# Output projection applied per head, with rows added into x + bo in DRAM by accumulating scatters

## The reference, cut to what matters

```
q, k, v = x @ Wq + bq, x @ Wk + bk, x @ Wv + bv           # 16 heads of 16
scores  = q @ k.T * 0.25                                  # 4096 x 4096 for each head
top     = top_k(scores.max(-1) - scores.mean(-1), 307)
sel     = softmax(q[top] @ k.T * 0.25) @ v                # 307 x 16 for each head
a       = zeros; a[top] = sel
x1      = layernorm(x + (a @ Wo + bo))
xr, xk  = mu_r*x1 + (1-mu_r)*prev(x1), mu_k*x1 + (1-mu_k)*prev(x1)
out     = layernorm(x1 + sigmoid(xr @ W_r.T) * (relu(xk @ W_k.T)**2 @ W_v.T))
```

## Time and profile before

| | us |
|---|---|
| median of 3 runs | 3275.21 |
| lowest and highest run | 3268.93, 3281.18 |
| span of the profiled execution | 3267.6 |
| busy in it: TensorE, VectorE, ScalarE, GpSimd | 2972.6, 2890.4, 2836.5, 1580.4 |

### The profile page before, as it was taken

The page is one execution under the profiler, slowest core; times in us unless marked ns, Lnnn a source line. Parts: engine busy times, 40 slices in busy tenths (PEclk is TensorE's granted clock), DMA queues, the critical chain, the costliest instruction groups (busy, mean ns, idle before and its releaser), DMA issues. The chain is left out here.

```text
span 3267.6 us, 57726 instructions
## 1 busy us (share of the span) xinstructions
PE 2972.6 (91%) x15364; PEld 1367.2 (42%) x15364; DVE 2890.4 (88%) x5704; ACT 2836.5 (87%) x6246; POOL 1580.4 (48%) x2787
## 2 busy tenths in 40 slices
PE   6999899998989999998999999899999899997688
PEld 3333333333433443443334444444444343444477
DVE  4999999999989998998999999899999898997567
ACT  5999889997988999899899888799988699895566
POOL 4223122224644553654355564766565663557754
PEclk8999999999999999999999999999999999998889
DMA  6334223342151131223121233122151023202022
GB/s 182 90 86 121 76 71 81 90 34 40 34 38 31 35 41 17 32 40 35 24 41 30 60 52 40 36 39 41 37 48 41 24 39 32 41 15 16 16 83 73
DMA packets 263603, 163.56 MB, mean 50 GB/s; under 512 B 168876, under 2 KB 242796, under 8 KB 259180
## 3 DMA queue, kind: packets, MB, share of 16 engines
q1 hardware_dynamic: 255180, 156.41, 25.8%
q0 software_dynamic: 6144, 1.37, 0.5%
q10 hardware_dynamic: 1952, 2.10, 0.2%
HBM read 111.86 MB, written 47.86 MB: 49 GB/s over the span
## 5 line engine op out<-in xcount | busy, mean ns | idle before, releaser
L1189 DVE CUSTOM_DVE_ANT_0 JK<-DP,AB 128x1024 bf16<-128x1024 f32 x2048 | 2463.1, 1222 | 239.8 <-DVE SPr L1189 91.5
L1033 ACT ACTIVATE AB<-CP 128x512 f32<-128x512 f32 x4096 | 2291.3, 622 | 201.0 <-PE CP L749 147.0
L768 PE MATMUL DP<-KS,QS 128*128 128x512 f16 x4096 | 1230.2, 382 | 61.5 <-DVE SPr L1189 53.9
L1641 POOL TENSOR_TENSOR SCR<-E 128x307 f16<-128x307 f32 x957 | 666.1, 709 | 516.3 <-ACT E L1068 509.2
L749 PE MATMUL CP<-KS,QS 128*128 128x512 f16 x2048 | 789.7, 386 | 57.4 <-ACT AB L1033 34.6
L758 PE MATMUL CP<-KS,QS 128*128 128x512 f16 x2048 | 790.4, 386 | 34.8
L768 PEld LDWEIGHTS DP<-KS,QS 128*128 128x128 f16 x4096 | 357.0, 99 | 357.9 <-DVE SPr L1189 171.5
L1068 ACT ACTIVATE E<-BP 128x307 f32<-128x307 f32 x904 | 430.5, 476 | 34.5 <-PE BP L860 31.3
L749 PEld LDWEIGHTS CP<-KS,QS 128*128 128x128 f16 x2048 | 197.5, 96 | 525.3 <-ACT AB L1033 460.3
L758 PEld LDWEIGHTS CP<-KS,QS 128*128 128x128 f16 x2048 | 196.8, 96 | 411.5 <-ACT AB L1033 376.2
L860 PE MATMUL BP<-QT,KA 128*128 128x307 f16 x904 | 267.2, 296 | 22.6 <-ACT QT L1060 19.0
(11 more groups left out here) (414 smaller groups left out, 3087.2 us busy)
## 6 DMA issues: line engine op xcount, KB each, us to landing
KS<-KTC SPq DMA_DIRECT2D x256, 128.0 KB, 4.6
QS<-QSC SPq DMA_DIRECT2D x512, 64.0 KB, 2.2
KA<-KTC SPq DMA_DIRECT2D x128, 128.0 KB, 4.0
QN<-SCR SPq DMA_DIRECT2D x16, 544.0 KB, 3.4
SCR<-in_L_attn_x SPq DMA_DIRECT2D x16, 512.0 KB, 5.0
AO<-E SPq DMA_DIRECT2D x16, 512.0 KB, 6.9
VF<-in_L_attn_x SPq DMA_DIRECT2D x64, 128.0 KB, 2.2
VF<-AO SPq DMA_DIRECT2D x64, 128.0 KB, 2.2
```

The source lines that it names most:

```text
L768: r = pe.matmul(o[:, 512 * j:512 * j + 512], qs, ks[j][:, 0, :], start=True, stop=True)
L1033: act.activation(AB[p % 3][:, 512 * j:512 * j + 512], BANK["C%d" % j], ACT.Abs).then_inc(ab_full, 1)
L1189: dve.tensor_tensor_reduce(out=JK[p % 2][:], in0=BANK["D%d" % u], in1=AB[p % 3][:], scale=1.0, scalar=0.0, op0=ALU.add, op1=ALU.max, accum ...
L1641: pool.tensor_tensor(EL[a % NE], E[a % NE][:], EH[a % NE], ALU.subtract).then_inc(el_g, 1)
```

## The change

- `Wo` is applied head by head. The two copies of 16 rows of `Wo` that a head needs (for the high and the low half of the value sums) are loaded to `WB` by the sync engine. `otr` becomes two steps `wo`. Part 0 brings the softmax sums into columns (three products with one column of the identity) and multiplies the last 51 rows with `WB`; VectorE takes the reciprocal and scales. Part 1 multiplies the first 256 rows, and ScalarE scales them.
- `put` adds rows of 256 numbers to `Y` in DRAM by three accumulating indirect DMAs. `Y` holds x + bo: copied from x by sixteen DMAs of 512 KB (`ycopy`, in the steps of the values of sequence 0) and added to by sixteen accumulating DMAs from GpSimd (`ybias`, in the sixteen steps that transpose sequence 1). No zeros are written.
- The value bias is added in the value products, by one more product with a matrix of ones.
- `feed` has no Wo: it reads `Y`, and an iteration has seven steps. The first norm uses the same statistics as the second (`BN_STATS`).
- The mixing is written as `prev + mu*(cur - prev)`, with one subtraction, from one ring `x1R` instead of three tiles. In the second `feed` both scalings of the norms move from VectorE to ScalarE, and the addition before the second norm moves from VectorE to GpSimd.

```diff
-                yield [("otr", g, j // NT, bank()), ("put", g, j // NT)]
+                yield [("wo", g, j // NT, 0, bank())]
+                yield [("wo", g, j // NT, 1, bank()), ("put", g, j // NT)]
...
-            products = [("f7", 7, (("f3", 4), ("f2m", 3)), ()), ("f6", 6, (("f2s", 3),), (("f8", 8),)),
-                        ("f6k", 6, (("f2r", 3),), (("f9", 9),)),
-                        None, ("f2", 2, (), (("f0", 0),))]
...
+            products = [("f7", 7, (("f3", 4),), ()), ("f6", 6, (("f8", 8),), ()), ("f6k", 6, (("f2r", 3),), (("f9", 9),))]
...
+                    pe.wait_ge(bv_pool, 1)
+                    pe.matmul(o[:, 0:D], onesh[:], bvr[:], start=True, stop=False)
+                r = products(o[:, 0:D], "v", t, slice(0, D), False, part, False)
...
-            def otr(g, hl, bank):
+            def wo(g, hl, part, bank):
                 hx = HEAD0[g] + hl
-                o = claim(bank)
-                pe.wait_ge(ot_act, hx + 1)
-                for c in range(3):
-                    r = pe.transpose(o[:, 64 * c:64 * c + 2 * DH + 1], OT[hx % 2][:, 128 * c:128 * c + 128],
-                                     ident[0:2 * DH + 1, 0:2 * DH + 1])
-                r.then_inc(ot_pe, 1)
-                owed[bank] = ((og_dve, hx + 1),)
-
-            def f1(b, t, bank, late):
-                k = NT * b + t
-                o = claim(bank)
-                pe.wait_ge(l_f[k % 3], 32 * (k // 3 + 1))
-                transposes(o, 2, lambda q: fao[k % 3][:, 128 * q:128 * q + 128], ident[:]).then_inc(f_t0, 1)
-                owed[bank] = ((f_at, k + 1),)
+                o, ot, w = claim(bank), OT[hx % 2], WB[0:2 * DH, hx % 2, :]
+                if part == 0:
+                    pe.wait_ge(ot_act, hx + 1)
+                    pe.wait_ge(l_wo[hx % 2], 32 * (hx // 2 + 1))
+                    for c in range(3):
+                        pe.matmul(o[:, D + c:D + c + 1], ot[:, 128 * c:128 * c + 128],
+                                  ident[0:2 * DH + 1, 2 * DH:2 * DH + 1], start=True, stop=True)
+                    pe.matmul(o[:, 0:D], ot[0:2 * DH, 256:384], w, start=True, stop=True).then_inc(wo_pe, 1)
+                    owed[bank] = ((og_dve, hx + 1),)
+                else:
+                    for c in range(2):
+                        r = pe.matmul(o[:, D * c:D * c + D], ot[0:2 * DH, 128 * c:128 * c + 128], w, start=True, stop=True)
+                    r.then_inc(wo_pe, 1)
+                    owed[bank] = ((og_act, hx + 1),)
...
+            def wo(g, hl, part, bank):
+                if part:
+                    hx = HEAD0[g] + hl
+                    act.wait_ge(wo_pe, 2 * hx + 2)
+                    act.wait_ge(rec_dve, hx + 1)
+                    after(act, l_o, 48 * hx)
+                    for c in range(2):
+                        r = act.mul(OG[c], BANK[bank][:, D * c:D * c + D], rec[:, c:c + 1])
+                    r.then_inc(og_act, 1)
...
+            def f3(b, t, late):
+                if late:
+                    k = NT * b + t
+                    r = frs[:, k % 2, :]
+                    after(act, f_o2, k - 3)
+                    after(act, f_t1, k - 3)
+                    act.wait_ge(f_r1, k + 1)
+                    act.activation(fx1[k % 4], fx[k % 4], ACT.Identity, scale=r[:, 0:1], bias=r[:, 1:2]).then_inc(f_x1, 1)
...
-            def otr(g, hl, bank):
-                hx = HEAD0[g] + hl
-                sv = BANK[bank][:, 0:192].rearrange("p (c d) -> p c d", c=3)
-                dve.wait_ge(ot_pe, hx + 1)
-                after(dve, og_dve, hx)
-                dve.reciprocal(rec[:], sv[:, :, 2 * DH])
-                q = seq.mark(dve.tensor_copy(osum[:], sv[:, :, 0:DH]))
-                dve.wait_ge(q_dve, q)
-                q = seq.mark(dve.tensor_tensor(osum[:], osum[:], sv[:, :, DH:2 * DH], ALU.add))
-                dve.wait_ge(q_dve, q)
-                after(dve, l_o[hx % 2], 48 * (hx // 2))
-                dve.tensor_tensor(OG[hx % 2][:], osum[:], rec[:].unsqueeze(2).broadcast_to([128, 3, DH]),
-                                  ALU.mult).then_inc(og_dve, 1)
+            def wo(g, hl, part, bank):
+                if part == 0:
+                    hx = HEAD0[g] + hl
+                    dve.wait_ge(wo_pe, 2 * hx + 1)
+                    after(dve, og_act, hx)
+                    dve.reciprocal(rec[:], BANK[bank][:, D:D + 3]).then_inc(rec_dve, 1)
+                    dve.wait_ge(rec_dve, hx + 1)
+                    after(dve, l_o, 48 * hx)
+                    dve.tensor_scalar(OG[2], BANK[bank][:, 0:D], rec[:, 2:3], None, ALU.mult).then_inc(og_dve, 1)
...
-                dve.tensor_tensor_reduce(out=fh[j], in0=BANK[bank][:, 0:D], in1=fx[k % 3], scale=1.0, scalar=0.0,
-                                         op0=ALU.add, op1=ALU.add, accum_out=fsum[:, j:j + 1]).then_inc(f_y, 1)
...
+                after(dve, f_r1, k - 1)
+                dve.wait_ge(l_f[k % 4], 16 * (k // 4 + 1))
+                stats(fx[k % 4], k % 2, k % 2, f_s1, k + 1)
...
+            def ybias(b, i):
+                pool.wait_ge(l_y, 256)
+                pool.dma_start(Y[b][512 * i:512 * i + 512, :].rearrange("(t p) c -> p t c", p=128),
+                               bob[:].unsqueeze(1).broadcast_to([128, 4, D]), accum_op=ALU.add).then_inc(l_yb, 16)
...
-                pool.wait_ge(og_dve, hx + 1)
-                pool.wait_ge(q_pool, seq.mark(pool.tensor_tensor(OG[i][:], OG[i][:], bv3, ALU.add)))
-                pool.wait_ge(l_z, 256)
-                for c, (_, w) in enumerate(CH):
...
+                pool.wait_ge(l_yb, 256)
+                after(pool, l_o, 48 * hx)
+                pool.wait_ge(q_pool, rows_at[hx])
+                for c in (2, 0, 1):
+                    w, k = CH[c][1], 3 * (hx % H) + c
+                    pool.wait_ge(og_dve if c == 2 else og_act, hx + 1)
                     pool.indirect_dma_start(
-                        out=AOr[b], out_offset=bass.IndirectOffsetOnAxis(ap=ixf[0:w, k:k + 1], axis=0),
-                        in_=OG[i][0:w, c, :], in_offset=None).then_inc(l_o[i], 16)
-
-            def f2m(b, t, late):
-                k = NT * b + t
-                j = k % 2
-                after(pool, f_x1, k - 1)
-                pool.wait_ge(f_y, k + 1)
-                pool.tensor_scalar(fnm[:, j:j + 1], fsum[:, j:j + 1], -1.0 / D, None, ALU.mult).then_inc(f_m1, 1)
+                        out=Y[hx // H], out_offset=bass.IndirectOffsetOnAxis(ap=idxt[0:w, k:k + 1], axis=0),
+                        in_=OG[c][0:w, :], in_offset=None, compute_op=ALU.add).then_inc(l_o, 16)
+
+            def rstd(q):
+                v, r = fmv[:, q, :], frs[:, q, :]
+                pool.wait_ge(q_pool, seq.mark(pool.tensor_scalar(r[:, 0:1], v[:, 1:2], EPS, None, ALU.add)))
+                pool.wait_ge(q_pool, seq.mark(pool.tensor_tensor(r[:, 0:1], r[:, 0:1], halfc[:], ALU.pow)))
+                return pool.tensor_scalar(r[:, 1:2], v[:, 0:1], r[:, 0:1], -1.0, ALU.mult, ALU.mult)
...
+                q = seq.mark(pool.tensor_tensor(fd[k % 2], cur, prv, ALU.subtract))
+                pool.wait_ge(q_pool, q)
+                for m, ca in enumerate((MR, MK)):
                     fm = (fm0, fm1)[m][k % 2]
                     for c in range(2):
-                        pool.tensor_scalar(fmp[m][:, c, :], prv[:, c, :], cols[:, cb.start + c:cb.start + c + 1], 0.0,
-                                           ALU.mult, ALU.add)
-                        i = pool.tensor_scalar(fm[:, c, :], cur[:, c, :], cols[:, ca.start + c:ca.start + c + 1], 0.0,
+                        i = pool.tensor_scalar(fm[:, c, :], fd[k % 2][:, c, :], cols[:, ca.start + c:ca.start + c + 1], 0.0,
                                                ALU.mult, ALU.add)
                     pool.wait_ge(q_pool, seq.mark(i))
-                    i = pool.tensor_tensor(fm, fm, fmp[m], ALU.add)
+                    i = pool.tensor_tensor(fm, fm, prv, ALU.add)
...
-            def azero(b, i):
-                sp.wait_ge(zeroed, 1)
-                sp.dma_start(AO[b][512 * i:512 * i + 512, :].rearrange("(t p) c -> p t c", p=128),
-                             zero.unsqueeze(1).broadcast_to([128, 4, D])).then_inc(l_z, 16)
+            def ycopy(b, i):
+                sp.dma_start(Y[b][512 * i:512 * i + 512, :], x[b][512 * i:512 * i + 512, :]).then_inc(l_y, 16)
...
+            def wl(hx):
+                h = hx % H
+                after(sp, wo_pe, 2 * (hx - 1))
+                for a in (0, DH):
+                    sp.dma_start(WB[a:a + DH, hx % 2, :], Wo[DH * h:DH * h + DH, :]).then_inc(l_wo[hx % 2], 16)
...
+                after(sp, f_x1, k - 3)
+                sp.dma_start(fx[k % 4], Y[b][128 * t:128 * t + 128, :]).then_inc(l_f[k % 4], 16)
```

(12 more changed lines are left out.)

257 lines of the change are left out of this document (92 added, 165 removed).

## The result

| | before | after |
|---|---|---|
| median of the runs on one chip, us | 3272.07 (3268.77 to 3281.18) | 3300.14 (3295.47 to 3306.01) |
| span of the profiled execution, us | 3267.6 | 3304.2 |
| last score step starts, us | 2968.4 | 3006.0 |
| from there to the end, us | 299.2 | 298.2 |

The ratio is 1.0086 (95% interval 1.0064 to 1.0107): the changed kernel is slower by 0.9%, 28 us. The time lies in the predicted range, but not where the forecast was (3274, no change). The profiled execution itself took 3306.01, the longest of the four.

A forecast was written before the change was run, and what follows sets the result against it. No single engine but the pace of the score steps was taken as the bound. Terms 49 - 29 + 4 - 30 + 0 + 5 = -1 against span 3267.6 gave 3266.6; with 7.6 carried over, 3274 us, range 3236 to 3312.

The forecast's parts named there:

- term 4: Second feed-forward, in the tail: a tile every 3.45 us instead of 4.35, a gain of 30 us (bounds -36 and -14).
- If the tile's period stays near 4: Second feed-forward: named sign of being wrong, against stores expected every 3.4 to 3.5 us.
- Rival C: Filling Y: GpSimd's accumulating DMAs take 67 us, splitting sequence 1's keys late; +30 us, 3304; chance 0.18.
- Rival D: Second feed-forward: GpSimd and VectorE hinder each other, tile 3.9 us; head ends cost 2.0; 3293 us; chance 0.20.
- Term 1: Head ends within the loop: a loss of 1.8 us for each of 27 heads, +49 us (bounds +24 and +65).
- rival B: Head ends cost 0.9 us, not 1.8, absorbed by ScalarE's and TensorE's slack; faster, 3249 us; chance 0.31.
- Term 2: First feed-forward: fewer steps in the loop, -24 us, and pace almost unchanged, -5; together -29 us (bounds -12 and -45).
- Term 5: Rest of the tail: fewer leftover attention steps -3, longer head ends, gathers and scatter +3; together 0 (bounds -5 and +8).
- terms 3 and 6: Values: one more product for each of 64 tiles, +4 us; filling Y: sixteen copies and sixteen accumulating DMAs, +5 us.

The follow-up runs named there:

- e6: Changed kernel with the W_k product before the W_r one in the second feed-forward: 3277.58 us, ratio 1.0027 to the kernel before.
- e7: Changed kernel, second feed-forward with the W_k product before the W_r one and GpSimd's first-norm part at the iteration's front: 3273.72 us, ratio 1.0016.
- e10: Changed kernel with part 0's softmax sums brought by three transposes instead of three one-column products: 3294.95 us, ratio 1.0063 to the kernel before.
- e11: Changed kernel with empty step between head-end parts, part 1 scalings on VectorE, W_k product and first norm first, softmax sums by transposes: 3246.28 us, ratio 0.9925.
- e4: Changed kernel with row scatters that overwrite Y instead of adding to it (different output): one execution, 3283.28 us.

## Why the prediction was wrong

By the terms of the sum, against the spans (3267.6 and 3304.2):

| term | predicted | measured |
|---|---|---|
| 1, head ends in the loop | +49 | +54: eight steps around each of 27, 304.2 to 358.6 |
| 2, first feed-forward, last stretch | -24 | -23: steps 1723 to 1793, 120.0 to 97.1 |
| 2, its pace, and the steps between head ends | -5 | +2: +7 where it stands alone, -5 beside attention |
| 3, values | +4 | +1: steps 120 to 221 and 445 to 541 |
| 4, second feed-forward | -30 | -7: last head's copy to the end, 166.7 to 159.9 |
| 5, rest of the tail | 0 | +6: end of loop to the last head's copy, 132.5 to 138.3 |
| 6, filling `Y` | +5 | +1: steps 221 to 300 |
| steps 0 to 120, not in the sum | 0 | +2 |
| sum | -1 | +36 |

**The step that failed is term 4.** I wrote that "with three engines at 3.0 to 3.25 I expect 3.45". That adds up each engine's work and asks only for the longest sum. The dependency from W_k's product through relu and square to W_v's product of the next iteration was there before, too, but hidden: the Wo products and the transposes of `AO` stood between the two on TensorE. The change took exactly these away. What is left is three products (2.6 us) and some 1.4 of ScalarE in a ring. It is shown by e6 and e7: the same work in another order runs at 3.58 and 3.47, and in e7 the stretch takes 139.4 us, 27 less than before. The 3.45 of the sum was thus right for an order in which VectorE alone sets the pace, and the order wasn't read. Of the 37 us between the sum and the measured time this term makes 23. "If the tile's period stays near 4" was one of the named signs of being wrong, and it is the one that came. A smaller slip is the 4.35 for a tile before: it is one of the longer intervals, the median of the 31 is 4.22, and with it the term would have been some 4 us smaller. What I should have asked of the order is what TensorE does between W_k's product and W_v's in the next iteration: in the changed kernel only two passes of transposes, 0.38 together.

That 3300 us lies within the range is luck: its upper end was there for rivals C and D, and neither of them made the loss.

**Rival D** named a slower tile (3.9, near the 4.00 measured) with the wrong mechanism. Contention is there: the subtraction of two SBUF inputs takes 0.61 us beside GpSimd's addition, and 0.76 in the kernel with W_k first, where the earlier trace rows have 0.42 for such an operation with GpSimd reading nothing. This agrees with the rule of the Trainium skill, page "SBUF — State Buffer", section "Who interferes with whom", that a VectorE instruction with two SBUF inputs contends with a GpSimd instruction that reads SBUF. But in the changed kernel VectorE isn't the bound, and e6, with the 0.76 in it, still runs at 3.58. Whether those tenths count at 3.47, where VectorE is 97% busy, isn't tested.

**Term 1** was right in kind and 10% too low, and rival B (0.9 for a head end) was wrong. The wait of L895 for VectorE is 0.46 (I had about 0.6), ScalarE's scalings do wait for L895, and two row maxima start 2.4 to 2.6 apart, about as written. What I mis-sized is TensorE in part 0: I put its product "0.38 later". It is 1.1 later (1.39 for 0.30), since three products of one column take 0.76 us. By e10 this alone changes nothing, because it lies beside the same VectorE chain; it counts once the parts are set apart (e11).

**Term 2** held for the steps it frees. Its pace did not get better. I haven't tested why those steps take 1.57 us instead of 1.55 (323.3 and 318.8 over 206); it stays open.

**The clock** is a rival that the prediction didn't have. The mean granted clock is 0.980 in the profile of before and 0.974 in that of the changed kernel. It can't make the loss at the head ends, which sum to 357.0 and 358.6 us in two executions whose clock in the loop was 1.00 and 0.99. But the same loop took 7 us less in the first of these, so some of the remaining microseconds in the table may be the clock's; no run sets it apart.

**Rival C** had the price nearly right, by another way than it named, and the effect wrong:

```profile
348.74 19.89 POOL L1516 DMA_DIRECT2D Y<-bob  x15
408.57 1.30 POOL L1516 DMA_DIRECT2D Y<-bob  x1 [39.94 <-issue]
409.54 1.42 POOL L1409 TENSOR_SCALAR SCR<-SCR 128x1024 f16<-128x1024 f32 x1
...
L1516 POOL DMA_DIRECT2D Y<-bob x16: 1302/4836/9015, 348.7 to 408.6; - x16
...
DMA to landing us min/median/max: 8.7/32.7/48.7
```

The recorded lengths of the accumulating DMAs of 512 rows (1.3 to 9.0 us) overlap and aren't their price: the first fifteen start 0.75 to 1.0 us apart, and together with the sixteenth they keep GpSimd busy for 21.2 us. But the sixteenth starts only at 408.57, 0.25 us after the landing of the fifteenth (it started at 359.62 and took the 48.7). It is so in every execution with these DMAs; why GpSimd can't issue it earlier isn't shown. So they hold GpSimd for 61 us, about the 67 of the rival, and hardly anything waited: the trace of before has GpSimd idle for 59.7 us in this place, waiting for VectorE's piece of the keys (its L1442 at 406.32). In the changed kernel's trace the first split of the keys (L1409) starts 0.2 us after that piece is ready, as before; in e6 it comes 1.8 us after it. The cover is larger than the 37 us that I priced, and just about what was needed. Steps 221 to 300 took 114.1 us instead of 113.1, and 113.2 in the changed kernel again.

**Term 5** is where accumulation is paid: 7 to 12 us by e4, of which I had 3. The +6 of the table is one pair of executions (132.5 and 138.3), and with the same work the stretch took 133.1 in e6, so +1 to +6 is all that is shown.

Two of the errors (terms 3 and 6) went the other way, by 7 us in all, and hide a part of the rest.

## What to carry to other kernels

When work is removed from a pipelined loop, it isn't enough that each engine's sum falls: look for what the removed instructions covered, which is the distance on that engine between a product and the next one that needs its result through other engines. Put the product with the longest way through other engines first in the iteration, and independent ones behind it. And when two waits lie on one chain, making one shorter lengthens the other: first set them apart by a step, then shorten each.

## What the runs showed of the hardware

- Three matrix products of one fp32 column with 33 rows of weights took 0.76 us, three fp32 transposes of 33 columns 0.30, each time from their start to that of the next matrix instruction at one head end. The trace records six instructions for the first (x6) and three for the second (x3): a product of one column isn't cheap.
- An accumulating scatter of 128 rows of 1 KB takes GpSimd 1.57 us in the median, the plain one 1.00 (e4); the scatter of 51 rows, the first of its three, takes 1.85 and 1.15 in the mean.
- An accumulating DMA of 512 KB from a broadcast SBUF source took 32.7 us to landing in the median, with fifteen in flight, and 8.7 us for the one issued alone (11.6 in the changed kernel again); a copy of the same size from DRAM to DRAM took 7.5. The loads of x took 7.1 in the median instead of 5.0; which of the new transfers did that isn't told apart.
- GpSimd issued fifteen of these accumulating DMAs 0.75 to 1.0 us apart and the sixteenth only 0.25 us after the fifteenth had landed, 40 us later, in the changed kernel and within 0.3 us in its other executions. The Trainium skill, page "DMA: Bandwidth & Descriptors", section "Anatomy of one DMA — SWDGE (gpsimd) path", calls descriptor generation on this path small and variable. The 0.75 us from one issue to the next agrees with small; the pause of 40 us before the sixteenth is no part of that account.
